# A perceiver block on one core: in the last batch of the first attention, sums, output-bank reading and two expert chunks put in another order

## The reference

```python
x = x + xattn(layernorm(x), ctx, ctx)        # 16 heads of 16; ctx is 8 x 1601 x 256
x = x + attn(layernorm(x))                   # causal self-attention over the 64 tokens of a batch
x = x + ffn(layernorm(x))                    # 8 experts, the 2 best of each token, weighted
# xattn: softmax(q k^T / 4) v, with q, k, v and output projections and biases
# ffn:   gelu(x W1[e] + b1[e]) W2[e] + b2[e] for every expert e, hidden width 1024
```

## Time and profile before

| | |
|---|---|
| median of 3 runs | 671.48 us (670.67 to 673.57) |
| the profiled execution | 674.92 us, its span 673.1 us |
| mean granted clock of PE | 0.989 |
| busy over the span | PE 647.2 us (96%), DVE 473.2 (70%), ACT 326.8 (49%), POOL 298.4 (44%) |
| last batch and what follows it | batch 7 from about 424 us; its denominators at 462.74; transpose `xt1` of the last tile at 471.06; experts alone from about 505 |

### The profile page before, as it was taken

The page is one execution under the profiler, slowest core; times in us unless marked ns, Lnnn a source line. Parts: engine busy times, 40 slices in busy tenths (PEclk is TensorE's granted clock), DMA queues, the critical chain, the costliest instruction groups (busy, mean ns, idle before and its releaser), DMA issues.

```text
span 673.1 us, 15769 instructions
## 1 busy us (share of the span) xinstructions
PE 647.2 (96%) x6408; PEld 533.3 (79%) x6408; DVE 473.2 (70%) x871; ACT 326.8 (49%) x533; POOL 298.4 (44%) x386
## 2 busy tenths in 40 slices
PE   7989999999999999999999999888999999999997
PEld 4778878778778868877886876657789999999997
DVE  4887767676759778476877864768778677667753
ACT  4355655654554554554455544345554444444431
POOL 2147787997766788596668757100000000000000
PEclk9999999999999999999999999878999999999999
DMA  5311110100110010110001000153003303320001
GB/s 177 135 50 50 39 39 26 51 26 25 27 50 2 26 52 25 26 51 25 27 25 26 1 2 1 33 220 127 1 1 126 115 12 125 125 98 26 0 0 33
DMA packets 13285, 34.12 MB, mean 51 GB/s; under 512 B 1563, under 2 KB 10532, under 8 KB 11044
## 3 DMA queue, kind: packets, MB, share of 16 engines
q1 hardware_dynamic: 13188, 33.19, 14.8%
q0 software_dynamic: 32, 0.01, 0.0%
HBM read 32.67 MB, written 0.52 MB: 49 GB/s over the span
## 4 chain that ended last, share of the span: by engine, by line
PE 79%; DVE 10%; issue 5%; POOL 3%; ACT 2%; DMA 0%; POOLq 0%; DVEq 0%; ACTq 0%
PE bank L1169 45%; PE bank L1363 9%; PE bank L1178 9%; PE bank L1349 4%; PE bank L1239 3%; POOL prob_sum L482 3%; PE bank L1282 2%; PE bank L1291 2%; DVE maxes L883 2%; DVE prob_sum L482 2%; DVE ctx_lo L466 1%; DVE shift L825 1%; ACT k_hi L618 1%; PE bank L1266 1%; DVE k_lo L864 1%
## 5 line engine op out<-in xcount | busy, mean ns | idle before, releaser
L482 POOL TENSOR_TENSOR prob_sum<-probs,prob_sum 128x256 f32<-128x256 f32 x336 | 268.5, 831 | 72.1 <-ACT probs L722 66.7
L722 ACT ACTIVATE probs<-bank 128x1024 f32<-128x1024 f32 (+1 forms) x104 | 106.7, 1026 | 115.3 <-PE bank L1363 103.2
L883 DVE TENSOR_REDUCE maxes<-bank 128x1 f32<-128x400 f32 (+1 forms) x256 | 129.5, 565 | 21.7 <-PE bank L1239 21.3
L704 ACT ACTIVATE h_raw<-bank,b_sb 128x512 f32<-128x512 f32 (+2 forms) x72 | 46.2, 642 | 107.0 <-PE bank L1169 106.9
L1169 PE MATMUL bank<-w_hi,h_hi 128*128 128x256 f32 x256 | 72.6, 284 | 0.0
L1169 PE MATMUL bank<-w_hi,h_lo 128*128 128x256 f32 x256 | 72.1, 282 | 0.0
L1169 PE MATMUL bank<-w_lo,h_hi 128*128 128x256 f32 x256 | 72.0, 281 | 0.0
L1178 PE MATMUL bank<-probs,v_sb 128*32 128x128 f32 (+1 forms) x1664 | 68.3, 283 | 2.5 <-DVE masked L815 2.0
L864 DVE SCALAR_TENSOR_TENSOR k_lo<-bank,bias_sb,k_hi 128x400 fp32r<-128x400 f32 (+2 forms) x64 | 40.4, 631 | 43.0 <-ACT k_hi L618 42.8
L1169 PE MATMUL bank<-wv_hi,ctx_hi 128*128 128x256 f32 (+1 forms) x208 | 65.4, 314 | 2.7 <-DVE maxes L883 2.4
L1363 PE MATMUL bank<-qbd_hi,k_hi 64*128 64x256 f32 (+1 forms) x416 | 67.9, 322 | 0.0
(11 more groups left out here) (158 smaller groups left out, 1422.0 us busy)
## 6 DMA issues: line engine op xcount, KB each, us to landing
raw<-in_w SPq DMA_DIRECT2D x16, 1024.0 KB, 6.8
ctx_raw<-in_ctx_t SPq DMA_DIRECT2D x16, 400.0 KB, 3.6
ctx_raw<-in_ctx_t SPq DMA_DIRECT2D x8, 402.0 KB, 3.6
ctx_raw<-in_ctx_t SPq DMA_DIRECT2D x8, 399.0 KB, 3.6
w_sb<-in_w_t SPq DMA_DIRECT2D x1, 1280.0 KB
w_raw<-in_w_t SPq DMA_DIRECT2D x2, 256.0 KB, 4.7
result<-x_all SPq DMA_DIRECT2D x4, 128.0 KB, 2.0
x_all<-in_x SPq DMA_DIRECT2D x1, 384.0 KB, 4.2
```

The source lines that it names most:

```text
L482: ins = engine.tensor_tensor(prob_sum[0:ROWS[k], cols], probs[0:ROWS[k], s % 2, cols], acc[0:ROWS[k]], ALU.add)
L704: nc.scalar.activation(h_raw[:, c % 2, 0:width], bank[:, at, 0:width], ACT.Gelu, bias=b1_sb[:, bass.ds(e, 1), c:c + 1].rearrange("p a b -> ...
L722: nc.scalar.activation(probs[0:ROWS[k], s % 2, :].rearrange("p (g n) -> p g n", g=G), bank[0:ROWS[k], score_bank(b, k):score_bank(b, k) + ...
L883: nc.vector.tensor_reduce(maxes[:, g * PAIRS + j, c:c + 1], src[:, 0:width], AX.X, ALU.max).then_inc(read_dve, 1)
```

## The change

Four edits, all around the last batch. On DVE, the sum of step k is added in step k+1 instead of step k (the last one at the end of step 12), and in step 1 the reading of the bank `O` of the batch before now stands ahead of the first sum. The table for the chain of tile 2 is moved: `y2`, `xt2` and `router` one step later, `gt` and `b2` three (two behind the router's own shift). On PE, the first two chunks of expert 0 are written before and behind the last weighing, ahead of the denominators, into banks 4 and 5 instead of 0 and 1; ACT's two gelus stand right behind the loading of the gelu table. The first `output` waits in addition until both gelus have read banks 4 and 5.

```diff
 CHAIN_AT_LAST = {2: ["y1"], 4: ["xt1"], 5: ["qk", "v"], 7: ["s0"], 8: ["st00", "st01"], 10: ["s1"],
-                 11: ["st10", "st11"], 12: ["o0", "o1"], 14: ["y2"], 16: ["xt2"], 17: ["router"], 19: ["gt"],
-                 20: ["b2"]}
+                 11: ["st10", "st11"], 12: ["o0", "o1"], 15: ["y2"], 17: ["xt2"], 18: ["router"], 22: ["gt"],
+                 23: ["b2"]}
...
-FIRST_HIDDEN = {0: [0, 1], 1: [2], 3: [3, 4], 9: [5, 6], 11: [7]}
+FIRST_HIDDEN = {1: [2], 3: [3, 4], 9: [5, 6], 11: [7]}
...
             use_table(ACT.Gelu)
+            for c in range(2):
+                gelu(0, c, c, 4 + c, DONE_TILES * P, False)
...
                     b = 2 * t + bi
-                    if more == bi == 1:
-                        sum_probabilities(nc.vector, dve, b, k, s, 1)
...
                         own_heads(bank[:, O, :], o_read, b)
+                    if more == bi == 1 and k > 0:
+                        sum_probabilities(nc.vector, dve, b, k - 1, s - 1, 1)
...
                         split_w(0, SPLIT_W_AT.index(k), SPLIT_W_AT.index(k))
+                    if more == bi == 1 and k == KT - 1:
+                        sum_probabilities(nc.vector, dve, b, k, s, 1)
...
             tile(TT - 1, LAST)
-            weigh(B - 1, 1, KT - 1)
-            denominators(B - 1)
...
+            pe.wait_ge(w_split, PIECES)
+            pe.wait_ge(xn2_split, DONE_TILES)
+            pe.wait_ge(read_act, TAIL.before[1])
+            pe.wait_ge(read_dve, TAIL.before[2])
+            hidden(0, 0, 4, 0, DONE_TILES)
+            weigh(B - 1, 1, KT - 1)
+            hidden(0, 1, 5, 0, DONE_TILES)
+            denominators(B - 1)
...
                     if c == 0:
                         pe.wait_ge(w_split, 2 * PIECES)
+                        pe.wait_ge(h_ready, 2)
                     output(0, c, c, 4, 0, DONE_TILES)
```

More of the change, by code:

```diff
@@ L1478, in _ @@
                 for c in FIRST_HIDDEN.get(s, []):
-                    if c == 0:
-                        pe.wait_ge(w_split, PIECES)
-                        pe.wait_ge(xn2_split, DONE_TILES)
                     if c >= 2:
```

## The result

| | before | after |
|---|---|---|
| median of 12 runs | 673.55 us (670.65 to 674.72) | 668.57 us (667.94 to 673.16) |
| ratio after to before | | 0.9948, 95% interval 0.9929 to 0.9967 |
| profiled execution | 674.92 us, span 673.1 | 668.32 us, span 666.5 |
| mean granted clock, profiled | 0.989 | 0.997 |

The kernel is faster by 0.52%, which is 3.5 us. The medians lie 5.0 us apart and the two profiled executions 6.6 us. The three numbers lie up to 3.1 us apart, and that turned out to be the subject of the study. The ratio is the one to go by: the kernel before has faster and slower executions, and a median of 12 of them depends on which it caught.

What follows compares the result with a forecast made beforehand. PE was taken as the bound, losing some 14 us between 430 and 471 to waits and low clock. `xt1` 6.8 us earlier less 0.6 for clock gave 6.2, taken as 6.0 off the median: 665.5 us, range 663.4 to 669.3.

Steps and rivals of the forecast that it cites:

- Reading ahead: On DVE, the output bank is read before the sums; PE's wait shrinks from 1.99 to 0.3 us, 1.7 us won.
- The chain of tile 2: In the last batch, moved later at no cost; `xt2` waits some 0.7 us, the 2.95 us gates' wait goes.
- Sums a step later: DVE stops waiting for fresh exponentials; last sum ends at 456.7, denominators 5.9 us earlier; PE waits 1.4 us at step 8.
- the short one: Half-clock spell of 3.4 us from about 460.5, mostly over the 1.3 us wait for `xt1`, costing 0.3 us.
- I take 6.0 us off the median: From 6.2 us off the profiled execution, 6.0 us were taken off the median, giving 665.5 us.
- all three spells: Half-clock spells of 3.4, 6.9 and 3.4 us between 430 and 471, each behind a PE wait, costing 6.8 us.
- fall in the middle: Rival: PE's many short waits bring low clock between 446 and 456; 667.5 to 669.3 us, chance 0.21.
- Nothing is won: Rival: waits only move because DVE bounds the batch; gain 0 to 2 us, 669.5 to 671.5 us, chance 0.12.
- The loop between the queues: Rival: DVE's sums, ACT's exponentials and `w_hi`, and DVE's `w_lo` delay each other; time 675 us, chance 0.06.
- The rule of the Trainium skill: PE idling briefly but often between matmul groups can swing between two clocks; would make 668.4 us likeliest.

Runs made afterwards that it cites:

- only_sums: Kernel before with only DVE's later sums and the output bank read ahead of them; median 670.46 us, ratio 0.9979.
- the moved `w_lo`: Changed kernel with DVE's eight `w_lo` pieces moved later; median 665.00 us without the early chunks, 666.42 us with them and 11 idle matmuls.
- only_chunks: Kernel before with only the two chunks beside the last weighing, with their waits and gelus; median 672.68 us, ratio 1.001.
- before_filler: Kernel before with 33 idle matmuls added in five waits of PE's last batch, order untouched; median 669.88 us, ratio 0.9966.
- sums_filler: Kernel of only_sums with 7, 4 and 7 idle matmuls ahead of `xt2`, the last weighing and the denominators; median 667.02 us.
- after_pool_lo: Changed kernel with DVE's eight `w_lo` pieces of expert 0 made by POOL instead; median 671.47 us.

## Why the prediction was right in the place and wrong in the size

**Right, step by step.** Reading ahead: forecast 0.3 us of wait, measured 0.37. The chain of tile 2: `xt2` 0.7, measured 0.85; no wait for the gates. Sums a step later: a wait at step 8 of 1.4 us, measured 1.38; `b2` 0.2, measured 0.30; last sum's end 456.7, measured 455.51 + 1.21 = 456.72. Denominators 456.85, measured 456.78 with a wait of 0.34 instead of 0.8. `y1`: a wait of 2.6 us, measured 2.53, and one spell, the short one, which begins in that wait at about 459.5 and not behind it. `xt1` near 464.5, measured 464.47, without the 1.3 us of wait that was forecast ahead of it. For the execution that was profiled, 6.2 us were forecast and 6.6 came (674.92 to 668.32).

That the times agree to a few hundredths is in part luck. PE had begun the stretch 0.5 us earlier than in the profile before. Counted from the denominators of batch 6, those of batch 7 were forecast at 456.85 - 427.90 = 28.95 us and came at 29.38, and `xt1` came 6.1 us earlier than before (43.16 to 37.07).

**Wrong: the last step, "I take 6.0 us off the median".** The 6.2 us were two terms of different kinds. The walk made afterwards puts the schedule alone, at full clock, at 2.4 us; the other 3.8 were low-clock time, 4.4 that the profiled execution had and 0.6 that the changed one would have. I took all three spells as a standing cost of the kernel before: "Each spell of low clock stands just behind such a wait." They are not, as a whole: by the table the kernel before loses (1 - 0.9935) x 466 = 3.0 us to the clock in the mean, the profiled execution (1 - 0.989) x 466 = 5.1 (43.16 - 38.18 = 5.0 in the profiles). The other side was too small: the changed kernel loses (1 - 0.9960) x 466 = 1.9 in the mean, where 0.6 was counted. So the clock gave 1.2 us in the mean where 3.8 were forecast, the schedule 2.5 (1.7 with the clock held), together 2.9 to 3.7, where the interval has 3.5. I had noted that the profiled execution lay above all runs shown, 3.4 us over their median, and took 0.2 us for it. It was the sign that the clock term was taken at three times its mean.

**The rivals.** The clock did not fall in the middle in either profile of the changed kernel, at step 8, though only two executions were looked at, and the run at 673.16 us and 0.988 was not. The median of 668.57 lies in this rival's range (667.5 to 669.3) without its mechanism having been seen, so that agreement is no support for it. "Nothing is won" is not true of the whole, but of two of the three edits taken alone. The loop between the queues did not show: DVE ran at 1.74 us a step. The rule of the Trainium skill that was weighed ("TensorE: Matmul & The Clock Gate", "A second HAM failure mode: psum-queue depth-cycling") agrees with only_sums, where three waits of 1.1 to 1.8 us went with two spells and the lowest mean clock of all kernels. It does not with the middle of the changed kernel, whose waits of 0.37, 0.85, 1.38 and 0.30 us were followed by no fall in either profile.

**What stays open.** The chunks beside the last weighing: 0 to 0.7 us gained in the changed kernel, a loss of 1.4 to 1.8 us (medians, and at clock 1.00) beside the moved `w_lo`. Why the same wait is followed by low clock in one execution and not in the next is not shown by any run, nor how often the spells of the kernel before are of the kind told of below, under "A fall while PE is busy": only two of its executions were profiled.

## What to carry to other kernels

Before a gain is computed from one profile, split it into schedule and clock: take the waits at full clock, walk them through, and see how the profiled execution's time and clock stand among the other runs. A part of the loss that comes and goes between executions may be credited only with its mean, and the changed kernel's own must be taken off at its mean too. Work taken out of the queue that sets the pace (here DVE's, moved to where DVE idles) is worth more than work put into the holes of the engine that waits.

## What the runs showed that was not expected

**The same wait, two outcomes.** PE's wait of 1.99 us for the output bank was followed by half clock in both profiles of the kernel before and by none in only_chunks; 2.95 us for the gates by 6.9 us of it in one and 3.2 in another.

**A fall while PE is busy.** Three of 12 runs of before_filler are 4.5 us longer at clock 0.991 (and three of sums_filler, 671.43 to 672.02 beside 666.3 to 667.5, none of which was profiled). Two windows of before_filler, whose profiled execution was one of them:

```profile
490.00:499.00 9.00, 8.27 (x65) 7.88 (x64) 6.47 (x22) 6.94 (x15) 0.00 (x0) 1.00 0.01 2
499.00:510.00 11.00, 11.00 (x51) 10.47 (x51) 5.51 (x18) 2.97 (x8) 0.00 (x0) 0.54 0.48 193
```

PE is busy for all of the 11 us from 499, in the first steps of the experts, and runs them at 0.54 of its clock; the last nine microseconds ahead of it had 0.7 us of idle time. It costs 4.9 us of the span: 206.93 us from `xt1` to the end where all other profiles have 202.0. No profile here shows what brings it on.

**DVE is slower by half beside POOL.** In after_pool_lo sums of 1.22 us took 1.9 on the mean while POOL subtracted, and single short operations took up to 1 us more. Three of them (1.05, 1.20 and 1.23 us) began inside one of POOL's pieces and ended with it, to 0.1 us; POOL's spans are rough, so that is a sign and no more. POOL's own pieces took 1.3 us each beside the short operations and 2.2 beside the sums (10.95 us for the last five).
